# A projection's bias moved from TensorE to VectorE, and two small gathers moved behind sixteen others

## The reference, cut to what matters

```python
h = (x @ W).reshape(n, HEADS, OUT_DIM)
a_src = jnp.einsum('nhc,hc->nh', h, att_src)
a_dst = jnp.einsum('nhc,hc->nh', h, att_dst)
e = jax.nn.leaky_relu(a_src[src] + a_dst[dst], NEG_SLOPE)
m = jax.ops.segment_max(e, dst, num_segments=n)
e = jnp.exp(e - m[dst])
denom = jax.ops.segment_sum(e, dst, num_segments=n)
alpha = e / (denom[dst] + 1e-16)
out = jax.ops.segment_sum(h[src] * alpha[:, :, None], dst, num_segments=n)
out = out.reshape(n, HEADS * OUT_DIM) + bias
```

## Time and profile before

| | |
|---|---|
| median of 3 runs | 3037.08 us (3033.0 to 3042.88) |
| the profiled execution's own time | 3038.42 us |
| its span, first to last instruction | 3036.6 us |
| mean granted TensorE clock | 0.918 |
| TensorE busy | 2533.4 us (83%) |
| VectorE busy | 1326.1 us (44%) |
| GpSimd busy | 1023.7 us (34%) |
| ScalarE busy | 736.1 us (24%) |

### The profile page before, as it was taken

How to read it: one execution, slowest core, us unless ns; L and a number is a source line. 1 busy time by engine, 2 the same in 40 slices (tenths; PEclk the granted TensorE clock), 3 DMA queues, 4 the chain that set the end, 5 groups by cost and what they waited for, 6 DMA issues and landing times.

```text
span 3036.6 us, 36289 instructions
## 1 busy us (share of the span) xinstructions
PE 2533.4 (83%) x10887; PEld 1675.6 (55%) x10888; DVE 1326.1 (44%) x3641; ACT 736.1 (24%) x1657; POOL 1023.7 (34%) x927
## 2 busy tenths in 40 slices
PE   3676789999979999999999998998977993278780
PEld 1333689447976555655565555897634452144440
DVE  7798676567860010201010003304546774255658
ACT  3566655113541000100010002663300001031102
POOL 0000047777773000000000000000468887787850
PEclk8899899999989999999999999999879996599985
DMA  7455579555437434344434441342159887466551
GB/s 250 195 206 217 185 233 284 156 156 162 132 105 190 159 127 156 130 152 129 156 130 150 130 155 47 88 130 59 38 137 299 253 250 229 126 177 180 173 161 42
DMA packets 227857, 488.35 MB, mean 161 GB/s; under 512 B 47609, under 2 KB 155438, under 8 KB 227438
## 3 DMA queue, kind: packets, MB, share of 16 engines
q1 hardware_dynamic: 129343, 290.75, 30.0%
q10 hardware_dynamic: 62319, 137.95, 14.1%
q0 software_dynamic: 36032, 57.60, 7.3%
HBM read 368.81 MB, written 117.36 MB: 160 GB/s over the span
## 4 chain that ended last, share of the span: by engine, by line
PE 58%; POOL 13%; DVE 13%; issue 6%; DMA 6%; ACT 2%; ACTq 0%; DVEq 0%; SPq 0%
PE banks L1377 27%; PE banks L908 11%; POOL features_and_rows L1841 11%; DVE features_and_rows L536 5%; PE banks L2228 4%; PE banks L1092 3%; PE banks L1107 3%; PE banks L1366 2%; PE banks L1352 2%; PE banks L554 2%; DVE pair_and_bias_rows L533 2%; DMA hidden<-table_counts 2%; POOL weights_b L1841 2%; DMA features_and_rows<-table_heads,src 1%; PE banks L1734 1%
## 5 line engine op out<-in xcount | busy, mean ns | idle before, releaser
L777 POOL DMA_INDIRECT table_dense_weights<-pair_weight,dst x416 | 409.0, 983 | 537.5 <-DVE node_of_last_rows L1002 383.5
L1377 PE MATMUL banks<-own_term,features_and_rows 128*128 128x391 f32 (+1 forms) x1664 | 551.9, 491 | 0.0
L1841 POOL DMA_INDIRECT features_and_rows<-table_heads,src x380 | 481.3, 1267 | 121.3 <-issue 106.8
L908 PE MATMUL banks<-split_rows,count_columns 128*128 128x256 f32 (+1 forms) x3750 | 487.5, 288 | 15.2 <-ACT count_columns L896 11.6
L908 PEld LDWEIGHTS banks<-split_rows,count_columns 128*128 128x128 f32 x3750 | 466.3, 193 | 19.6 <-issue 10.6
L1377 PEld LDWEIGHTS banks<-own_term,features_and_rows 128*128 128x128 f32 x1664 | 314.9, 189 | 232.5
L1415 DVE TENSOR_SCALAR features_and_rows<-banks,hop_bias 128x391 f32<-128x391 f32 (+1 forms) x24 | 15.0, 625 | 901.9 <-PE banks L1377 901.9
L2228 PE MATMUL banks<-features_and_rows,edge_to_window 128*128 x880 | 264.0, 458 | 152.1 <-DVE edge_to_window L2190 130.6
L2228 PEld LDWEIGHTS banks<-features_and_rows,edge_to_window 128*128 128x128 f32 x880 | 158.3, 210 | 257.6 <-issue 242.5
L554 PE MATMUL banks<-features_and_rows,pair_and_bias_rows 128*128 128x400 f16 x806 | 199.1, 394 | 110.5 <-DVE features_and_rows L536 53.3
L1377 PE MATMUL banks<-features_and_rows 128*128 128x391 f32 (+1 forms) x832 | 277.8, 491 | 0.0
(11 more groups left out here) (415 smaller groups left out, 2693.9 us busy)
## 6 DMA issues: line engine op xcount, KB each, us to landing
hidden<-table_counts SPq DMA_DIRECT2D x305, 160.0 KB
table_dense_weights<-weights_c ACTq DMA_DIRECT2D x26, 1600.0 KB, 5.6
own_term<-table_dense_weights SPq DMA_DIRECT2D x52, 782.0 KB, 4.3
own_term<-table_dense_weights SPq DMA_DIRECT2D x52, 780.5 KB, 4.2
features_and_rows<-table_rows_by_edge SPq DMA_DIRECT2D x52, 528.0 KB, 3.9
pair_and_bias_rows<-table_edge_rows ACTq DMA_DIRECT2D x52, 512.0 KB
weights_c<-table_edge_rows ACTq DMA_DIRECT2D x52, 512.0 KB
table_rows_by_edge<-features_and_rows SPq DMA_DIRECT2D x43, 528.0 KB, 5.4
```

Of the source, the lines that this page charges most:

```text
L777: e.indirect_dma_start(out=self.table, out_offset=bass.IndirectOffsetOnAxis(ap=self.place[:, t:t + 1], axis=0), in_=self.values[:, t:t + 1 ...
L908: m = e.matmul(to[:, 0:wide], lhs_of(k), piece(k, h, wide), start=(k == first and h == 0), stop=False, skip_group_check=True)
L1377: m = e.matmul(psum[b][:, 0:wide], z_block(block)[:, f * P:(f + 1) * P], streamed[tile % STREAM][:, lo:lo + wide], start=False, stop=(bloc ...
L1841: e.indirect_dma_start(out=to[:, k, :], out_offset=None, in_=t_h, in_offset=bass.IndirectOffsetOnAxis(ap=src[:, t:t + 1], axis=0)).then_in ...
```

## The change

The one-row product is taken out; the last product of a tile now ends the sum in the bank. The two copies on ScalarE become a tensor-tensor addition and a copy on VectorE. The bias rows in `brow` are loaded to all 128 partitions already. The second edit moves the two gathers of the scan-row values from ahead of the first quad to behind the fourth.

```diff
                 for k in range(K_IN):
                     m = T(lambda e, ps=ps, j=j, k=k: e.matmul(ps[:, 0:DIM + 2 * HEADS], xT[:, k, j * P:(j + 1) * P],
-                                                              w3[:, k, :], start=(k == 0), stop=False),
+                                                              w3[:, k, :], start=(k == 0), stop=(k == K_IN - 1)),
                           freed, turned_ok[j])
-                m = T(lambda e, ps=ps: e.matmul(ps[:, 0:DIM], ones[0:1, :], brow[0:1, B_ATT, :], start=False, stop=True), biases)
-                A(lambda e, ps=ps, j=j: e.copy(h_rows[:, j, :, 0:HEAD_DIM], heads(ps[:, 0:DIM])), m, ones_ok)
-                reader[i] = cp = A(lambda e, ps=ps, j=j: e.copy(
+                V(lambda e, ps=ps, j=j: e.tensor_tensor(h_rows[:, j, :, 0:HEAD_DIM], heads(ps[:, 0:DIM]), heads(brow[:, B_ATT, :]),
+                                                        ALU.add), m, biases, ones_ok)
+                reader[i] = cp = V(lambda e, ps=ps, j=j: e.tensor_copy(
                     a_both[:, :, j, :], ps[:, DIM:DIM + 2 * HEADS].rearrange("p (r h) -> p r h", h=HEADS)))
...
         def gather_rows(e):
-            e.wait_ge(*w_pair)
-            e.wait_ge(*row_first_known)
-            for c in range(2):
-                e.indirect_dma_start(out=first_value[:, c:c + 1], out_offset=None, in_=t_pair,
-                                     in_offset=bass.IndirectOffsetOnAxis(ap=row_first[:, c:c + 1], axis=0)).then_inc(s_first_value, 16)
             e.wait_ge(*w_h)
             for n in range(STAGED):
                 d = n % DIRECT
                 if n >= DIRECT:
                     e.wait_ge(s_kept_rows[d], 16 * (n // DIRECT))
                 gather_group(e, STAGED_QUADS[n], staging[d], s_staged[d])
+                if n == 3:
+                    e.wait_ge(*w_pair)
+                    e.wait_ge(*row_first_known)
+                    for c in range(2):
+                        e.indirect_dma_start(out=first_value[:, c:c + 1], out_offset=None, in_=t_pair,
+                                             in_offset=bass.IndirectOffsetOnAxis(ap=row_first[:, c:c + 1], axis=0)).then_inc(s_first_value, 16)
```

## The result

The changed kernel took 3002.7 us (median of 4 runs, 2996.7 to 3005.9); the kernel before, run beside it, 3035.8 (4 runs, 3033.0 to 3042.9). The ratio on record is 0.9885, 95% interval 0.9861 to 0.991 (the quotient of the two medians alone is 0.9891). Forecast were 3012 and a range of 3003 to 3027: the direction and the mechanism came true, the size lies 9 us further and 0.3 us outside the range.

What follows compares the result with a forecast made beforehand. GpSimd's chain of gathers behind the projection was taken to set the end; starting at 2217 instead of 2242.48, 25.5 us earlier, it turned 3038.4 into 3012.9, a median of 3012, with 8 in 10 for 3003 to 3027.

Steps and rivals of the forecast that it cites:

- That GpSimd's chain sets the end: Behind the projection, GpSimd's chain of gathers sets the end; the gain is how much earlier it starts, 25.5 us.
- Whether the clock rises: In the projection, without the one-row product, TensorE's clock rises about two tiles into a cold group.
- The group's length: A cold group's projection on TensorE takes 6.5 us where 13.01 stood, or 8.4 if the clock stays low.
- The additions on VectorE: Bias additions and copies on VectorE in the projection: 0.55 us a tile, 2.2 a group of four.
- The fast steps: Projection steps at full clock end on VectorE and take 13.8 us instead of 14.87.
- The scatters: GpSimd's last 18 scatters run from 2190 at 1.27 us each, plus 3 if slowed, leaving GpSimd free at 2217.
- The values: Scan-row values fetched behind 16 row gathers at 1.3 to 2 us each; node values land at 2220, without a wait.
- The sum: GpSimd's chain starts at 2217 instead of 2242.48, 25.5 us earlier, with the same instructions behind it; median 3012.
- mean does not change: As many gathers as before run beside VectorE's scan, so their mean time stays the same.
- The clock did not stay low: Rival, 22 in 100: TensorE's clock stays low in the projection; gain 17 us, time 3020.
- The early gathers: Rival, 12 in 100: GpSimd's early gathers crawl at 2.2 us instead of 1.3; gain 8 to 15, 3022 to 3029.
- The clock did not fall in the fast steps: Rival, 10 in 100: TensorE's clock falls there; 3023 to 3029 for one step lost, up to 3046 for three.

Runs made afterwards that it cites:

- e15: The changed kernel with 32 small operations of GpSimd's own ahead of its first row gather; ratio to the kernel before 0.9934.
- e5: The changed kernel with 12 further row gathers on GpSimd ahead of the first quad, their rows fetched twice; ratio to the kernel before 0.9954.
- e3: The kernel before with the one-row product replaced by the identity times 128 rows of the bias; ratio to the kernel before 0.9905.
- e12: The changed kernel with the one-row product kept and VectorE's addition made a plain copy; ratio to the kernel before 0.9996.
- e6: The kernel before with the bias product 128 rows high and the scan-row gathers moved; ratio to the kernel before 0.9896, again 0.9901.
- e7: The changed kernel with VectorE's evictions put behind the next step's normalization and lengths; ratio to the kernel before 0.9887, again 0.9896.
- e4: The changed kernel with the bias left out altogether and both evictions on ScalarE; ratio to the kernel before 0.9859.
- e13: The kernel before with only the two scan-row gathers moved, run a second time; ratio to the kernel before 0.9975.

## Why the prediction was wrong in size and right in mechanism

The step that failed is the price of a group in the stage around the projection, and it is a matter of size: two terms, the products L1734 and the additions on VectorE, were priced too high. By these, group 4's first scatter came 4.5 us sooner than forecast. The waits, the order and the path were as forecast. How this and the scatter of the runs make up the 9 us is told under *The sum*.

*That GpSimd's chain sets the end*: right. e15 and e5 show it by adding a known amount, and over the kernels of the table the time follows the start within the intervals or within 1 us of them, but for the gathers alone.

*Whether the clock rises*: right, and in group 0 at the place forecast. Group 0 takes 5.62 us: two tiles at 1.87 and two at 0.935, twice the speed (16 products of group 1 take 2132.63 - 2128.89 = 3.74). The reason given, that the one-row product is all that these stretches have and others have not, is shown by e3 and e12. In group 4 the clock came back later, in the third tile, and the group took 6.6 us (2168.36 to 2174.97, the end of its products), still less than the up to 7.4 in the sum.

*The group's length*: mis-sized, the first of two terms. I priced L1734 at 2.1 and 1.12 us a tile, from rows in which it stands between one-row products. Alone it takes 1.87 and 0.935. So a fast one-row product cost 1.74 - 0.935 = 0.8 us a tile and not 0.62, and group 0 ended 0.9 us sooner than forecast, group 4 some 0.8 and group 5 0.9.

*The additions on VectorE*: mis-sized, the second term. I took 0.55 us a tile between bounds of 0.42 and 0.59; it was 0.41, at the lower bound (though the copy does not hide whole: 0.33 and 0.08). The fast steps, forecast at 13.8, took 2162.91 - 2149.70 = 13.2, two of them 1.2 us less. That over "the groups that are exposed" this is "under 1 us either way" holds of the distance between the bounds only. As the cost of the additions it would be too little: taking the evictions off VectorE's path is worth 3 to 8 us of the start (e6, e7, e4). The sum held that cost in its steps of 13.8 and in what it put behind the projection of group 5, so the total did not suffer.

*The scatters*: right as a sum. I forecast 26.2 us from the first scatter of group 4 to the start (18 at 1.27 and 3 for the slowed ones); it was 2213.51 - 2187.28 = 26.2. Four beside VectorE's first steps of the expansion took 1.63 to 1.85.

*The values*: right. 16 gathers took 21.4 us, 1.34 each, the values landed 28.4 us after their issue at 2190.8, and nothing waited.

*The sum.* Forecast was a start of 2217 - 2114.4 = 102.6 against 98.1 measured: 4.5 us, of which the first scatter of group 4 has all (76.4 forecast, 71.9 measured). The terms above make up nearly all of it: 0.9, 0.8 and 0.9 from the products of groups 0, 4 and 5, and 1.2 from the two fast steps; the rest of some 0.7 lies in rounded terms. With that the gain would have been 30 and the forecast 3007. The kernel before was 1.3 us faster in the set of the result than in that of the forecast. The remaining 3 us have no cause that a trace shows; they are within what two sets of runs of the same pair differ by. That is a third fault, of the range and not of the sum: its lower end of 3003 stood for scatters that nothing slows and a clock kept through groups 4 to 6. Neither came, and the result still lies 0.3 us below it, because the range held nothing for the scatter of sets of few runs. It is a matter of luck on which side of 3003 one set falls: the mean of the change's two ratios, 0.9897, gives 3004.5 with the same kernel before. That the gathers' "mean does not change" was nearly so: the first eight intervals of the row gathers shrank from 17.4 to 10.1 us, as they run while VectorE still waits, but the chain from the first gather of any kind to the last row gather fell only from 695.5 and 690.9 (two traces) to 687.1 and 691.3.

*The rivals.* The clock did not stay low (0.72 and 1.00 above, not 0.50). The early gathers did not crawl: 1.34 us each. The clock did not fall in the fast steps: 1.00 with TensorE busy for 81% of the stretch and idling 1.4 us ahead of each group. The Trainium skill (TensorE: Matmul & The Clock Gate, "A second HAM failure mode: psum-queue depth-cycling") tells of an oscillation under frequent short idle pieces between groups of products; in the fast steps here the trace shows none.

## What to carry to other kernels

A product that fills one row of the array to add a bias costs more than its columns: look at the granted clock of the stretches that hold it, and if it stays low while TensorE is never idle, give the row to another engine, or simply multiply the identity by the bias on all rows. An eviction moved to the engine that ends the step is paid in everything queued behind it there, so move it only for what it frees, and place it behind the work that others wait for (here that moved the start by 6 us; in time it was not clear of the noise). Time an issuing engine's chain from a fixed event of the same execution, not from the launch, and put the scatter of small sets of runs into the range.

## What the runs showed of the hardware

- With a one-row f32 product of 2 x 256 columns in each tile, TensorE busy for all of 13.01 us kept a granted clock of 0.50 (before, e12). Where the clock was up already, the same mix did not lower it (before, groups 1 to 3, 7 us each between other products: 1.00). With the same columns 128 rows high it rose in the group's second tile, begun 2.8 us after the first (e3). At full clock a tile takes 0.935 us without a bias product, 1.35 with the one 128 rows high and 1.74 with the one-row product: for the same columns the single row costs 0.8 us and the full height 0.4.
- A gather's own time on GpSimd stretches to VectorE's operation beside it: 4.05 us beside one of 3.62 in e15, where a quiet one takes 0.95. It began 0.39 us behind VectorE's operation and ended 0.82 us behind its end. The Trainium skill (SBUF — State Buffer, "SBUF: two separate sides") says that one of the two holds the port pair for its whole instruction; the trace agrees.
- The same write of the node values took from 17.7 us (e7) to 38.5 us (e13) to land, at otherwise nearly the same place of the program. Work placed behind such a write wants a margin of that size.
